# Two attention branches and a mixture of experts in one kernel: scores on halves of TensorE's array, masks of the maxima in 32x32 blocks, splits on GpSimd, tasks in another order

## The chip, the cores and the metric

One NeuronCore of a Trainium2 chip runs the whole program. The metric is the time of one execution on the device in microseconds. Its engines are called as in the profile: PE (TensorE, matmuls) with PEld (its weight loads), DVE (VectorE), ACT (ScalarE), POOL (GpSimd) and SP (SyncE, which here only issues DMAs). Each engine runs its own list of instructions in order; semaphores tie the lists together.

## The reference

The input x is 32 sequences of 256 rows of 128 float32. Two branches start from the layer norm of x and are added to x:

```python
xn = _layernorm(x)
# branch one: 16 heads of 8, causal, with biases
scores = jnp.einsum('bhqd,bhkd->bhqk', q, k) / SCALE
scores = jnp.where(causal_mask, jnp.float32(-1000000000000.0), scores)
attn = jnp.einsum('bhqk,bhkd->bhqd', softmax(scores), v); ... attn @ Wm + bm
# branch two: rmsnorm, 16 heads of 64 (32 of them rotated, keys from a latent of 16), causal
att = jnp.einsum('bhqd,bhkd->bhqk', q, k) / jnp.sqrt(jnp.float32(D))
y = softmax(att) @ v @ Wo; x1 = xn + y
# and behind it, on the rmsnorm of x1, a mixture of experts: top 2 of 8, plus a shared one
out = x + branch_one + (x1 + shared + routed)
```

Both softmaxes need the largest score of each query, so the scores are computed twice: once for their maximum and once for the exponential, the maximum then being taken off by two more rows of the contraction.

## The kernel before

A *block* is one sequence of 256 rows; there are 32 (`NB`). A loop over `c` runs from -1 to NB + 2, and in each turn over twelve *steps* `k`. In turn c PE makes the maxima's scores of block c + 1 and the exponentials' scores of block c: steps 0 to 5 are the six units of branch one, steps 6 to 11 the six of branch two. A unit (`UNITS`) is a pair of a 128-key tile and a 128-query tile for eight heads, 128 x 1024 scores in two PSUM banks; four of six are diagonal and need the causal mask. MX (`psm`) is the one buffer for the maxima, EX (`pse`) the one for the exponentials.

What each engine does in a step:

- PE: `max_unit` into MX (after DVE has read the last one, semaphore s_mr), some task, `exp_unit` into EX (after ACT's exponential of the last one, s_pt), more tasks; after every third step 24 matmuls `pv_half` of probabilities and values into PV (`psv`), which already use four column quarters of the array.
- DVE: the maximum over MX, which also transposes in 32x32 blocks (`max_unit`, L734), and tasks.
- ACT: the exponential of EX into PT (L1100), and ahead of a diagonal unit it writes the mask into EX, a bank at a time (a *seed*, L1106, semaphore s_sd counts them), on which the scores are then accumulated; and tasks.
- POOL and SP: tasks and DMAs.

The tasks are all the rest: projections of block c + 2 (`prep_*`), normalisation and output of block c - 1 (`norm`, `tail_in`, `tail_out`), and the experts for pairs of blocks (`moe_*`), so that even and odd turns differ. Their place is written out by hand as `if k == ...` in each engine's loop, the same for all turns. Three PSUM banks `ps0` to `ps2` are given out in turn (`claim`); `arrived` and `released` wait for a bank to be filled or freed.

Numbers are carried in parts. Branch one splits q and k in three bf16 parts, stacked as 48 rows of the contraction: `qsA`, `ksA` are [98, 16 heads, 256], of which 48 rows are parts, 48 are zeros and two carry the maximum. One matmul per head is 128 keys by 128 queries, eight per unit. Branch two uses float32r and two parts: `qsB` [128, 16, 256] holds high and low parts of the queries; a unit is, per bank, one 512-column product with the keys' high part (`ks1`, or `ksm` with 32 extra rows that mask a diagonal tile in the maxima) and one with their low part (`ks2`). The maxima of branch two go by 32 queries and all heads (`WIDE`). The mask of branch one's maxima is a matmul of an identity and the mask, 512 columns per bank, on four units of six (`mask`).

DVE splits the keys (`prep_ks`) and the experts' input (`moe_split`); POOL copies the keys into ksm (`prep_km`). The stacks of A and B are made by a write to DRAM and reads from it (`stack_a`, `stack_b`, `read_b`).

Of the kernel before, what the change touches and what calls it, by code (L numbers as in the profile page):

```python
# [14 lines left out]
H = 16  # L15
# [6 lines left out]
WIDE = [(0, 0), (0, 2), (0, 4), (0, 6), (1, 4), (1, 6)]  # L22
# [24 lines left out]
def build(nc, I, out, NB):  # L47
    with ExitStack() as ctx:
# [3 lines left out]
        def sem(name):  # L52
# [8 lines left out]
        qsA = [sb(f"qsA{i}", [98, H, S], BF16) for i in range(2)]  # L61
        ksA = [sb(f"ksA{i}", [98, H, S], BF16) for i in range(2)]
        qsB = [sb(f"qsB{i}", [128, H, S], F32R) for i in range(2)]
        ks1 = [sb(f"ks1{i}", [98, S], F32R) for i in range(2)]
        ksm = sb("ksm", [128, 4, 128], F32R)
        same = sb("same", [32, S], F32R)
        ks2 = [sb(f"ks2{i}", [98, S], F32R) for i in range(2)]
# [5 lines left out]
        R1 = [sb(f"R1{i}", [128, H, 4]) for i in range(2)]  # L73
        negm = [sb(f"negm{i}", [128, 32]) for i in range(2)]
# [7 lines left out]
        kcs = sb("kcs", [96, 2, S])  # L82
# [6 lines left out]
        wkk = sb("wkk", [128, 2, 192], F32R)  # L89
# [18 lines left out]
        kt_ = sb("kt_", [96, 2, S])  # L108
# [22 lines left out]
        scrA = [nc.dram_tensor(f"scrA{i}", (3, 2, 128, S), BF16).ap() for i in range(2)]  # L131
# [9 lines left out]
        d_mk = sem("d_mk")  # L141
# [18 lines left out]
        s_half, s_zq, s_zk, s_k1, s_ksi, s_wa, s_wn, s_wb, s_sa, s_sb = (  # L160
            sem(n) for n in ("s_half", "s_zq", "s_zk", "s_k1", "s_ksi", "s_wa", "s_wn", "s_wb", "s_sa", "s_sb"))
# [9 lines left out]
        sqk, sx, skk = stage[:, 0:256], stage[:, 256:768], stage[:, 768:960]  # L171
# [40 lines left out]
        def _(e):  # L212
# [15 lines left out]
            def scores(br, b, bk, u, i, K, start):  # L228
# [3 lines left out]
                if br == 0:  # L232
                    for j in range(4):
                        h = h0 + 4 * i + j
                        t = mm(bk[:, i, 128 * j:128 * j + 128], ksA[s][0:K, h, keys], qsA[s][0:K, h, queries], start and j == 0, True)
                else:
                    o = bk[:, i].rearrange("p (h q) -> p h q", h=4)
                    r = qsB[s][0:K, h0 + 4 * i:h0 + 4 * i + 4, queries]
                    mm(o, ks1[s][0:K, keys], r, start, False)
                    t = mm(o, ks2[s][0:K, keys], r, False, True)  # L240
                return t

            def wide_scores(b, u, i):

                s, (kt, q0) = b % 2, WIDE[u]
                keys, queries = slice(128 * kt, 128 * kt + 128), slice(32 * (q0 + i), 32 * (q0 + i) + 32)
                o = MX[:, i].rearrange("p (h q) -> p h q", h=H)
                if kt == q0 // 4:
                    mm(o, ksm[:, (q0 + i) % 4], qsB[s][:, :, queries], True, False)
                else:  # L250
                    mm(o, ks1[s][0:96, keys], qsB[s][0:96, :, queries], True, False)
                return mm(o, ks2[s][0:96, keys], qsB[s][0:96, :, queries], False, True)

            def max_unit(br, b, u):
                g = unit(br, b, u)
                if g >= 1:
                    w.wait_ge(s_mr, g)
                if br == 0:
                    if b or u >= 3:
                        w.wait_ge(d_ar[b % 2], 192 * (b // 2 + 1))  # L260
                    else:
                        w.wait_ge(d_a0, 192)
                else:
                    for hh in range(2):
                        w.wait_ge(d_br[b % 2][hh], 112 * (b // 2 + 1))
# [1277 lines left out]
```

## Time and profile before

| | us |
|---|---|
| median of 3 runs | 1465.03 (1463.62 to 1465.06) |
| the profiled execution | 1464.32 |
| its span, first to last instruction | 1462.3 |
| busy: PE, DVE, ACT, POOL | 1376.2, 1146.6, 997.3, 587.5 |
| mean granted clock of PE | 0.978 of full |
| DMA | 155.86 MB, mean 107 GB/s |

A span is measured from the first to the last instruction of the program, the execution's own time has a little around it. Busy time is the union of an engine's instructions; since matmuls overlap, how often PE issues them is read from the distance of their starts in the timeline, not from their durations.

### The profile page before, as it was taken

The page shows a single profiled execution, that of the slowest core. Times are in us where ns is not written, and L with a number is a line of the kernel's source. Part 1 is how long each engine was busy: PE and PEld are TensorE (multiplying, and loading weights), DVE is VectorE, ACT ScalarE, POOL GpSimd, SP SyncE. Part 2 cuts the span into 40 slices and gives each one's busy share as a digit, 9 for nine tenths or more (in the row PEclk, how much of TensorE's full clock was granted, in tenths as well). Part 3 has the DMA queues.
Part 4 walks back from the last instruction along what each step waited for, and adds up shares of the span by engine and source line. Part 5 has one row for each costly group of instructions (what it writes and reads, how often), then busy time and mean ns, then how long its engine had stood idle before and what let it go on. Part 6 is the DMA issues. An engine that isn't in the chain of part 4 may idle for free.

```text
span 1462.3 us, 36231 instructions
## 1 busy us (share of the span) xinstructions
PE 1376.2 (94%) x14438; PEld 1073.2 (73%) x14438; DVE 1146.6 (78%) x2358; ACT 997.3 (68%) x1585; POOL 587.5 (40%) x610
## 2 busy tenths in 40 slices
PE   4689999999999999999999999999999999999985
PEld 3467777777877777787777777777777777777653
DVE  7877797978879797987979788797879879787613
ACT  2156777767777777777777777777776777777762
POOL 5323434354433434443343445334344534433112
PEclk9589999999999999999999999999999999999997
DMA  6666655645465565556556545655655465555100
GB/s 161 122 124 122 122 118 108 129 100 115 85 129 116 115 120 107 115 91 118 115 114 119 112 110 96 112 120 113 116 114 113 102 101 119 116 106 115 17 3 14
DMA packets 136677, 155.86 MB, mean 107 GB/s; under 512 B 32687, under 2 KB 126543, under 8 KB 127391
## 3 DMA queue, kind: packets, MB, share of 16 engines
q1 hardware_dynamic: 118078, 151.97, 51.5%
q10 hardware_dynamic: 18432, 1.58, 1.6%
q8 instruction: 115, 1.88, 0.6%
q14 instruction: 52, 0.42, 0.1%
HBM read 82.79 MB, written 67.11 MB: 103 GB/s over the span
## 4 chain that ended last, share of the span: by engine, by line
PE 69%; DVE 18%; ACT 8%; issue 4%; POOL 0%; DMA 0%; ACTq 0%; DVEq 0%
PE ps L217 22%; PE psm L217 16%; PE pse L217 15%; PE psv L217 10%; DVE R L734 5%; ACT PT L1100 3%; DVE rt L796 2%; PE ps L325 2%; ACT pse L1106 2%; DVE th L846 1%; PE ps L391 1%; DVE xs L662 1%; ACT th L1179 1%; DVE th L858 1%; ACT th L1148 1%
## 5 line engine op out<-in xcount | busy, mean ns | idle before, releaser
L734 DVE TRANSPOSE_TENSOR_REDUCE R<-psm 128x32 f32<-128x1024 f32 x384 | 478.7, 1247 | 133.3 <-PE psm L217 132.2
L1100 ACT ACTIVATE PT<-pse 128x1024 f32<-128x1024 f32 x384 | 392.3, 1022 | 210.4 <-PE pse L217 210.3
L1106 ACT ACTIVATE pse<-maskb 128x512 f32<-128x512 bf16 x510 | 285.4, 592 | 16.9 <-ACT PT L1100 6.2
L217 PE MATMUL pse<-qsB,ks 98*128 98x512 f32 x768 | 215.0, 402 | 8.0 <-ACT pse L1106 7.8
L1296 POOL TENSOR_TENSOR ts_<-ts_,pA 128x512 f32<-128x512 f32 x32 | 37.2, 1162 | 445.8 <-DVE pA L668 445.8
L217 PE MATMUL psm<-qsB,ks 96*128 96x512 f32 x512 | 180.6, 414 | 6.0 <-DVE R L734 6.0
L217 PEld LDWEIGHTS pse<-qsB,ks 98*128 98x128 f32 x768 | 137.1, 189 | 58.6 <-issue 18.9
L1304 POOL TENSOR_TENSOR tc_<-tc_,ts_ 128x512 f32<-128x512 f32 x64 | 82.3, 1286 | 190.4 <-DVE ts_ L688 190.4
L217 PE MATMUL pse<-qsA,ksA 98*128 98x128 bf16 x1536 | 127.0, 220 | 9.7 <-ACT pse L1106 8.4
L217 PEld LDWEIGHTS psm<-qsA,ksA 96*128 96x128 bf16 x1536 | 96.3, 100 | 51.9 <-issue 27.7
L217 PE MATMUL psm<-qsA,ksA 96*128 96x128 bf16 x1536 | 120.9, 223 | 13.3 <-DVE R L734 12.6
L217 PEld LDWEIGHTS pse<-qsA,ksA 98*128 98x128 bf16 x1536 | 94.8, 98 | 39.8 <-ACT PT L1100 16.4
L217 PE MATMUL psm<-qsB,ksm 128*128 128x512 f32 x256 | 110.9, 433 | 9.5 <-DVE R L734 9.5
L217 PEld LDWEIGHTS psm<-qsB,ks 96*128 96x128 f32 x512 | 94.5, 192 | 22.0 <-DVE R L734 7.5
L1334 POOL TENSOR_TENSOR hT<-th,cbs 128x512 f32<-128x512 f32 x64 | 81.9, 1280 | 70.3 <-ACT cbs L1168 69.2
L1116 ACT ACTIVATE OT<-psv 128x512 f32<-128x512 f32 x128 | 76.5, 598 | 46.7 <-PE psv L217 46.7
L217 PE MATMUL ps<-xs,wqx 128*128 128x256 f32 x576 | 95.5, 303 | 8.0 <-DVE wqx L868 7.3
L1309 POOL TENSOR_TENSOR pB<-tc_,pB 128x1024 fp32r<-128x1024 f32 x32 | 76.2, 2380 | 58.4 <-ACT pB L1090 58.4
L217 PE MATMUL psv<-PT,vA 128*9 128x128 f32 x3072 | 97.1, 275 | 0.0
L217 PE MATMUL psv<-PT,vB 128*17 128x128 f32 x3072 | 96.4, 274 | 0.0
L217 PEld LDWEIGHTS ps<-xs,wqx 128*128 128x128 f32 x576 | 82.0, 196 | 15.7 <-DVE wqx L868 7.5
L217 PEld LDWEIGHTS psv<-PT,vB 128*17 128x17 f32 x3072 | 78.4, 97 | 15.5 <-issue 12.3
(194 smaller groups left out, 2623.7 us busy)
## 6 DMA issues: line engine op xcount, KB each, us to landing
scrB<-pB SPq DMA_DIRECT2D x32, 1536.0 KB, 6.0
qsB<-scrB SPq DMA_DIRECT2D x384, 128.0 KB
scrA<-pA SPq DMA_DIRECT2D x32, 384.0 KB, 2.8
qsA<-scrA SPq DMA_DIRECT2D x186, 64.0 KB
ksA<-scrA SPq DMA_DIRECT2D x186, 64.0 KB
xs<-in_x SPq DMA_DIRECT2D x16, 256.0 KB, 9.0
out<-zz SPq DMA_DIRECT2D x16, 256.0 KB, 4.7
qsB<-same SPq DMA_DIRECT2D x64, 16.0 KB
```

The source lines that it names most:

```text
L217: return e.matmul(o, l, r, start=start, stop=stop, skip_group_check=True)
L325: t = e.transpose(bk[:, c:c + 128], OT[n % 2][:, 256 * a + 128 * qt:256 * a + 128 * qt + 128], ident[:])
L391: t = e.transpose(bk[:, c:c + 128], BT[:, qt, 128 * a:128 * a + 128], ident[:])
L734: e.tensor_reduce(red, MX[:].rearrange("p i (c q) -> p (i c) q", q=32), AX.X, ALU.max, apply_transpose=True).then_inc(s_mr, 1)
L796: e.tensor_tensor(DD, L, bl(rs[:, 3], 8), ALU.subtract).then_inc(s_dd, 1)
L1100: e.activation(PT[g % 4], EX[:], ACT.Exp, scale=(8.0 ** -0.5, 0.125)[br]).then_inc(s_pt, 1)
L1106: e.activation(EX[:, i].rearrange("p (h q) -> p h q", h=4), bc(maskb[:], 4), ACT.Copy).then_inc(s_sd, 1)
L1116: e.activation(OT[n % 2][:], PV[:], ACT.Copy).then_inc(s_ot, 1)
L1296: e.tensor_tensor(rA[:], fA[:], pA[:, 0], ALU.subtract).then_inc(s_ra, 1)
L1304: e.tensor_tensor(tc_[:, a], tc_[:, a], ts_[:, a], ALU.add).then_inc(s_tr, 1)
L1309: e.tensor_tensor(pB[:, 1, 1:3], rot, pB[:, 0, 1:3].bitcast(F32), ALU.subtract).then_inc(s_pb2, 1)
L1334: e.tensor_tensor(hT[:, f, :], th[f % 2][:], cbs[f % 2][:], ALU.mult).then_inc(s_h, 1)
```

## The change

- **Branch one.** `qsA` and `ksA` become [128, 8, 256]: heads of one bank stand on rows 0 to 49, those of the other on rows 64 to 113, the zeros are gone. `pair_scores` issues, for each of four head positions, one matmul on rows 0.. into bank 0 and one on rows 64.. into bank 1. The number of matmuls and their 128 columns stay. `exp_one` waits for both seeds ahead of its first matmul.
- **Masks of the maxima.** The two 512-column matmuls with a full identity become eight with 32x32 pieces of it, 32 x 4 x 32 each: only the diagonal 32x32 blocks are masked. What lies above them is masked after the maximum, by two additions of a table `later` in DVE's `join_max`.
- **Branch two.** `ks1` and `ksm` get 128 rows (keys' high part twice, for both parts of q), with the extra rows in gaps. The low products contract over 48 rows, those of bank 0 on rows 0.., of bank 1 on rows 64... In a step PE now issues `max_two`, `exp_two` (high products), then `max_low`, `exp_low`. The maxima go by 64 queries and eight heads per bank; on a diagonal tile the high product is two matmuls of 256 columns a bank.
- **POOL** takes the sum of `kt_`, the split of the keys and `moe_split` from DVE; `prep_km` is two copies of 48 rows.
- **DMAs.** Stack A is written by four and read by 16 DMAs a block (one and 12 before); branch one's row of maxima goes out in four DMAs from ACT (two before).
- **Order.** Nearly all tasks have other places. `pv_half(1, c - 1, 1)` goes ahead of the first scores of a turn, the others behind the step's tasks.

```diff
+            def pair_scores(b, bk, u, K, start):
...
+                for j in range(4):
+                    for i in range(2):
+                        rows = slice(64 * i, 64 * i + K)
+                        t = mm(bk[:, i, 128 * j:128 * j + 128], ksA[s][rows, h0 // 2 + j, keys], qsA[s][rows, h0 // 2 + j, queries],
+                               start and j == 0, True)
+            def max_one(b, u):
...
+                if diagonal:
+                    w.wait_ge(s_wa, WMASK)
                     for i in range(2):
+                        o = MX[:, i].rearrange("p (h g q) -> p h g q", h=4, g=4)
+                        for j in range(4):
+                            r = slice(32 * i, 32 * i + 32)
+                            mm(o[32 * j:32 * j + 32, :, j, :], identb[r, r], bc(maskb[r, r], 4), True, True)
+                pair_scores(b, MX, u, 48, not diagonal).then_inc(s_mx, 1)
+            def exp_one(b, u):
...
+                if diagonal and g:
+                    w.wait_ge(s_sd, 2 * seeds(g))
+                pair_scores(b, EX, u, 50, not diagonal).then_inc(s_ex, 1)
+            def max_two(b, u):
...
+                    if kt == q0 // 2:
+                        for j in range(2):
+                            mm(o[:, :, j, :], ksm[:, 2 * (q0 % 2) + j], r[:, :, j, :], j == 0, False)
+                    else:
+                        mm(MX[:, i].rearrange("p (h q) -> p h q", h=8), ksm[:, 4], qsB[s][:, 8 * i:8 * i + 8, 64 * q0:64 * q0 + 64], True, False)
+            def exp_two(b, u):
...
+                for i in range(2):
+                    if kt == qt:
                         w.wait_ge(s_sd, 2 * seeds(g) - 1 + i)
+                    h = 8 * i + h0 // 2
+                    mm(EX[:, i].rearrange("p (h q) -> p h q", h=4), ks1[s][:, 128 * kt:128 * kt + 128],
+                       qsB[s][:, h:h + 4, 128 * qt:128 * qt + 128], kt != qt, False)
+            def low_products(b, bk, kt, heads, queries):
+                s = b % 2
+                for i in range(2):
+                    r, h = slice(64 * i, 64 * i + 48), slice(8 * i + heads.start, 8 * i + heads.stop)
+                    t = mm(bk[:, i].rearrange("p (h q) -> p h q", h=heads.stop - heads.start), ks2[s][r, 128 * kt:128 * kt + 128],
+                           qsB[s][r, h, queries], False, True)
...
             def join_max(br, b):
                 w.wait_ge(s_mr, unit(br, b, 5) + 1)
+                if br == 0:
+                    w.wait_ge(d_w[2], 64)
+                    e.tensor_tensor(R0[0][:, :, 0:4], R0[0][:, :, 0:4], bc(later[:], H), ALU.add)
+                    step(e.tensor_tensor(R1[0][:], R1[0][:], bc(later[:], H), ALU.add))
+                    after()
...
+            def prep_ks(b):
...
+                step(e.tensor_copy(ks1[s][0:112, :], kt_[:, 0]))
+                e.tensor_tensor(ks2[s][:], kt_[:, 0], ks1[s][0:112, :].bitcast(F32), ALU.subtract).then_inc(s_ks, 1)
...
+                    if k == 9:
+                        if body:
+                            pv_half(1, c, 0)
                         if even and moe:
                             moe_g(p, 0)
```

PE around steps 4 to 6 of an even turn, before. `ps<-ident,OT` are the transposes of `norm`, `wqx` those of `prep_rope`, `wvA` of `prep_v`:

```order
L217 MATMUL psm<-qsA,ksA 128x128 x7
L217 MATMUL psm<-maskb,identb 128x512 x2
L217 MATMUL ps<-xs,wqx 128x256 [waits s_free0]
L217 MATMUL ps<-xs,wqx 128x256 x5
L217 MATMUL pse<-qsA,ksA 128x128 [waits s_sd,s_pt]
L217 MATMUL pse<-qsA,ksA 128x128 x3
L217 MATMUL pse<-qsA,ksA 128x128 [waits s_sd]
L217 MATMUL pse<-qsA,ksA 128x128 x3
L217 MATMUL ps<-wvA,xs 128x256 [waits s_free2]
L217 MATMUL ps<-wvA,xs 128x256 x3
L217 MATMUL psm<-qsB,ksm 128x512 [waits s_ks,d_br11,s_km,d_br10,s_mr]
```

And now:

```order
L221 MATMUL ps<-wvA,xs 128x256 x3
L221 MATMUL psm<-maskb,identb 32x4x32 [waits s_mr]
L221 MATMUL psm<-maskb,identb 32x4x32 x7
L221 MATMUL psm<-qsA,ksA 128x128 x8
L221 MATMUL pse<-qsA,ksA 128x128 [waits s_sd,s_pt]
L221 MATMUL pse<-qsA,ksA 128x128 x7
L221 MATMUL ps<-xs,wqx 128x256 [waits s_free0]
L221 MATMUL ps<-xs,wqx 128x256 x5
L221 MATMUL psm<-qsB,ksm 128x8x32 [waits d_br11,s_km,d_br10,s_mr]
```

The projection that stood between the maxima's and the exponentials' scores of step 5 is now behind both, `prep_v` ahead of both, and the second wait for a seed is gone.

PE in steps 7 and 8 of the same turn, before:

```order
L217 MATMUL pse<-qsB,ks 128x512 [waits s_pt]
L217 MATMUL pse<-qsB,ks 128x512 x3
L217 MATMUL ps<-xs,wqx 128x256 [waits s_free2]
L217 MATMUL ps<-xs,wqx 128x256 x5
L411 MATMUL ps<-ident,th 128x128 [waits s_x2,s_free1]
L411 MATMUL ps<-ident,th 128x128 x3
L325 MATMUL ps<-ident,OT 128x128 [waits s_ot,s_free0]
L325 MATMUL ps<-ident,OT 128x128 x3
L217 MATMUL psm<-qsB,ks 128x512 [waits s_mr]
```

And now (`psm<-qsB,ks` is `max_low`; of `pse<-qsB,ks` the first two rows are `exp_two`, the last `exp_low`):

```order
L439 MATMUL ps<-ident,th 128x128 x3
L221 MATMUL psm<-qsB,ksm 128x512 [waits s_mr]
L221 MATMUL psm<-qsB,ksm 128x512
L221 MATMUL pse<-qsB,ks 128x512 [waits s_sd,s_pt]
L221 MATMUL pse<-qsB,ks 128x512 [waits s_sd]
L221 MATMUL psm<-qsB,ks 128x512 x2
L221 MATMUL pse<-qsB,ks 128x512 x2
L353 MATMUL ps<-ident,OT 128x128 [waits s_ot,s_free2]
```

The low products of both buffers stand together at the end of the step, and one high product stands behind each wait for a seed where two matmuls stood before.

POOL in an even turn, before, from `moe_x` to `prep_rlo`:

```order
L1328 TENSOR_TENSOR rs<-rs,half 128x4 [waits s_ms]
L1329 TENSOR_TENSOR th<-yy,rs 128x512 [waits s_g]
L1273 TENSOR_TENSOR sm<-sm,half 128x2 [waits s_st2]
L1304 TENSOR_TENSOR tc_<-tc_,ts_ 128x512 [waits s_free0,s_g]
L1315 COPY ksm<-ks 96x512 [waits s_mx]
L1309 TENSOR_TENSOR pB<-tc_,pB 128x1024 [waits s_pb1]
```

And now:

```order
L1374 TENSOR_TENSOR rs<-rs,half 128x4 [waits s_ms]
L1375 TENSOR_TENSOR th<-yy,rs 128x512 [waits s_g]
L1334 TENSOR_TENSOR tc_<-tc_,ts_ 128x512 [waits s_free0]
L1359 COPY ksm<-ks 48x512 [waits s_mx]
L1360 COPY ksm<-ks 48x512 [waits s_g]
L1368 TENSOR_TENSOR zz<-zz,yy 128x256 [waits s_y,s_free1,s_km]
L1370 TENSOR_TENSOR zz<-zz,crow 128x256 [waits s_g]
L1334 TENSOR_TENSOR tc_<-tc_,ts_ 128x512 [waits s_free0]
L1379 CAST x<-aT 128x512 [waits s_free1]
L1380 TENSOR_TENSOR x2lo<-aT,x 128x512 [waits s_g]
L1343 TENSOR_TENSOR kt_<-kt_ 112x256 [waits s_free2]
L1339 TENSOR_TENSOR pB<-tc_,pB 128x1024 [waits s_pb1]
```

The two rotations, the tail and the experts' split (`x`, `x2lo`) now follow each other in this stretch.

## Rows read from the trace of the kernel before

**Rows 1.** The page: busy times, TensorE's granted clock, the chain by engine.
```profile
PE 1376.2 (94%) x14438; PEld 1073.2 (73%) x14438; DVE 1146.6 (78%) x2358; ACT 997.3 (68%) x1585; POOL 587.5 (40%) x610
...
PEclk9589999999999999999999999999999999999997
...
PE 69%; DVE 18%; ACT 8%; issue 4%; POOL 0%; DMA 0%; ACTq 0%; DVEq 0%
```
**Rows 2.** Who waited for whom: total us, times, the longest.
```profile
ACT PT L1100 <- PE pse L217: 210.3, 273, 12.6
...
DVE R L734 <- PE psm L217: 132.2, 121, 2.7
...
PE psm L217 <- DVE R L734: 28.1, 34, 5.4
```
**Rows 3.** Timeline of PE: start, us to the end, instruction, count, [idle before].
```profile
404.51 2.18 PE L217 MATMUL ps<-hT,wds 64*128 64x512 f32 x4
...
489.37 0.69 PE L217 MATMUL ps<-hT,wds 64*128 64x512 f32 x1
```
**Rows 4.** Timeline of PE in steps 4 to 6, 9, and a mask.
```profile
423.25 0.61 PE L325 MATMUL ps<-ident,OT 128*128 128x128 f32 x4
423.69 0.61 PE L217 MATMUL psm<-qsA,ksA 96*128 96x128 bf16 x8
424.14 0.60 PE L217 MATMUL psm<-maskb,identb 128*128 128x512 bf16 x2
...
425.91 0.72 PE L217 MATMUL ps<-wvA,xs 128*128 128x256 f32 x4
...
427.95 1.17 PE L217 MATMUL pse<-qsB,ks 98*128 98x512 f32 x4 [0.25 <-ACT pse L1106]
...
439.28 1.08 PE L217 MATMUL pse<-qsB,ks 98*128 98x512 f32 x4
440.29 1.51 PE L217 MATMUL psv<-PT,vB 128*17 128x128 f32 x48
441.73 0.51 PE L217 MATMUL psm<-qsB,ksm 128*128 128x512 f32 x1
442.07 0.40 PE L217 MATMUL psm<-qsB,ks 96*128 96x512 f32 x1
...
713.68 0.60 PE L217 MATMUL psm<-maskb,identb 128*128 128x512 bf16 x2
714.11 0.60 PE L217 MATMUL ps<-wmA,aT 128*128 128x128 f32 x4
```
**Rows 5.** Groups of instructions: busy us, mean ns, idle before them.
```profile
L1106 ACT ACTIVATE pse<-maskb 128x512 f32<-128x512 bf16 x510 | 285.4, 592 | 16.9 <-ACT PT L1100 6.2 <-issue 1.2
...
L217 PEld LDWEIGHTS psm<-qsA,ksA 96*128 96x128 bf16 x1536 | 96.3, 100 | 51.9 <-issue 27.7 <-DVE R L734 20.6
...
L217 PEld LDWEIGHTS psm<-qsB,ks 96*128 96x128 f32 x512 | 94.5, 192 | 22.0 <-DVE R L734 7.5
L1304 POOL TENSOR_TENSOR tc_<-tc_,ts_ 128x512 f32<-128x512 f32 x64 | 82.3, 1286 | 190.4 <-DVE ts_ L688 190.4
...
L217 PEld LDWEIGHTS psv<-PT,vB 128*17 128x17 f32 x3072 | 78.4, 97 | 15.5 <-issue 12.3
...
L738 DVE TENSOR_TENSOR R<-R 128x64 f32<-128x64 f32 x64 | 25.5, 399 | 2.2
...
L721 DVE TENSOR_TENSOR ks<-kt_,ks 96x256 fp32r<-96x256 f32 x32 | 13.5, 421 | 1.1
```
**Rows 6.** Timeline of ACT: step 2 with the row's DMAs, and step 5.
```profile
416.19 1.02 ACT L1100 ACTIVATE PT<-pse 128x1024 f32<-128x1024 f32 x1
...
417.33 1.12 ACT L1106 ACTIVATE pse<-maskb 128x512 f32<-128x512 bf16 x2
...
426.17 1.00 ACT L1100 ACTIVATE PT<-pse 128x1024 f32<-128x1024 f32 x1
427.21 1.12 ACT L1106 ACTIVATE pse<-maskb 128x512 f32<-128x512 bf16 x2
```

More of the change, by code:

```diff
@@ L287, in exp_unit @@
                     w.wait_ge(s_pt, g)
[L288 removed]
+                w.wait_ge(d_c[0], 64 * (b + 1))
                 diagonal = UNITS[u][0] == UNITS[u][1]
[L290 to L294 removed]
+                if diagonal and g:
+                    w.wait_ge(s_sd, 2 * seeds(g))
@@ L525, in _ @@
                             setup_row()
+                    now += 0.5
+                    if k == 0 and body:
+                        join_max(1, c)
                     if k == 1:
-                        if soon:
-                            prep_x(n2)
-                        if odd and moe:
-                            moe_c(p)
-                        if before:
-                            norm(1, c - 1, 1)
-                    if k == 2:
+                        if even and done:
+                            moe_d(p - 1, (2, 3))
                         if before:
@@ L537, in _ @@
                             moe_g(p, 4)
-                    if k == 3 and before:
-                        tail_out(c - 1)
-                    if k == 4 and soon:
-                        prep_nope(n2)
-                    if k == 5 and soon:
-                        prep_rope(n2, 0)
-                    if k == 6 and n1 < NB:
-                        join_max(0, n1)
-                    if k == 8 and odd and moe:
-                        moe_g(p, 2)
+                    if k == 2:
+                        if even and done:
+                            moe_t(p - 1)
+                        if soon:
+                            prep_qk(n2)
+                        if before:
+                            tail_out(c - 1)
@@ new lines, in _ @@
+                    if k == 3:
+                        if n1 < NB:
+                            prep_k2(n1)
+                        if soon:
+                            prep_nope(n2)
+                        if body:
+                            pv_half(0, c, 0)
+                    if k == 4 and body:
+                        norm(0, c, 0)
+                    if k == 5 and odd and moe:
+                        moe_sel(p, 0)
+                    if k == 6:
+                        if body:
+                            pv_half(0, c, 1)
+                        if n1 < NB:
+                            join_max(0, n1)
@@ L613, in _ @@
                             moe_d(p, (4, 0))
+                        if even and moe:
+                            moe_c(p)
         @block.vector
@@ L1254, in _ @@
+                        if even and moe:
+                            moe_c(p)
         @block.gpsimd
```

620 lines of the change are left out of this document (311 added, 309 removed).

## The prediction

> **What bounds the kernel now.** I read the page first. PE is busy 94% of the 1462.3 us span, DVE 78%, ACT 68%, POOL 40%, and the chain of waits that ended last lies on PE for 69% [rows 1]. The granted clock is at 2.4 GHz in nearly all slices, so it is no term here. The waits view then says who waits: ACT for PE 210 us before the exponentials, DVE for PE 132 us before the maxima, PE before its maxima only 28 us for DVE [rows 2]. So TensorE sets the pace, and ACT and DVE follow with some slack. The timeline gives the period: two equal places two blocks apart start at 404.51 and 489.37, so a block takes 42.4 us [rows 3]; there are 32, with a short start and end around them. I work per block and multiply by 32.
>
> Matmuls overlap, so I go by the distance of starts. Eight branch-one matmuls of 128 columns take 0.45 us (423.69 to 424.14), 0.056 each; two 512-column mask matmuls 0.43 (713.68 to 714.11), 0.22 each; a 512-column one of branch two 0.235 (four in 1.01 at 439.28, with a hole of 0.07 to 0.09 at the end, below), one of 256 columns half of that, 0.118 [rows 4].
>
> **The change part by part.**
>
> *Scores of branch one.* A block has 96 of them (12 steps of 8), 96 x 0.056 = 5.4 us. They now contract over 48 or 50 rows, and each two stand in different halves of the array with different banks. Bounds: the two of a pair run together (48 x 0.056 = 2.7 us, saving 2.7) or one after the other (saving nothing). No row shows row halves. The nearest one shows column quarters: 48 matmuls of PV take 1.44 us (440.29 to 441.73), 0.030 each, where the same kind unpacked takes 0.11 (four OT transposes 423.25 to 423.69) [rows 4]; so four did run together. I take together: -2.7.
>
> *Masks of the maxima.* Four steps a block have two 512-column matmuls, 4 x 0.43 to 0.44 = 1.76 us. Now eight of 32x128 each in eight different blocks of the array. By PV's 0.030 each that is 0.24 a step, and if all eight stream together little over 0.06. I take 0.15: -1.76 + 0.6 = -1.2 (bounds -0.8 and -1.5).
>
> *Low products of branch two.* A block has 24 (ks2), 24 x 0.235 = 5.6 us; in pairs 12 x 0.235 = 2.8 if together. -2.8 (bound: 0). The high products keep their columns: on the four diagonal maximum steps four of 256 (0.47) stand for two of 512 (0.47).
>
> Sum of matmul work: -6.7 us.
>
> *Switches.* This is what the change pays with. Whenever the array goes from whole to parts or back, the trace shows a hole. Four of 512 columns before PV take 1.01 instead of 0.94 (439.28 to 440.29), and PV's twelve rounds of four, at OT's 0.11 a round, take 1.32 of its 1.44 [rows 4]. So 0.07 to 0.12; I take 0.09 each way, and the same for row parts as for column parts. In the order a block now has some 34 such changes against 9: each of six branch-one steps has full to (mask to) pairs to full, each of six branch-two steps full to low pairs to full. 25 x 0.09 = +2.3 us. The page "TensorEngine Tiling (Array Packing)" of the Trainium skill, Key Properties, says that a change of tiling mode, not of tile, drains the engine. By that rule masks (32x32) and pairs (64x128) are two modes and pay a change between them, which no row here shows; without it the sum would be 4 x 0.09 = 0.4 us better.
>
> *Loads uncovered.* After a hole the first weight load is not hidden. After PV the step from ksm to ks takes 0.34 instead of 0.24 (441.73 to 442.07): 0.10 [rows 4]. Loads of bf16 are short and add about 0.01. Entries into full mode with a 4-byte load and into low pairs rise from 3 to some 18 a block: +1.6. The second load of a low pair may stand behind the first: 6 x 0 to 0.11; I take +0.3. Together with the switches: +4.2, so PE's own work falls by 2.5 us.
>
> *Waits on ACT.* EX is one buffer: last score matmul, exponential, two seeds, next scores. The trace has it bare: last matmul of a step at 425.85 (0.056 before 425.91), exponential at 426.17, seeds from 427.21, each 0.59 and the two in 1.12, PE goes on at 427.95, 0.15 after the first seed [rows 4 to 6]. That is 2.1 us for one seed and 2.6 for both. Branch one waited for one seed before its first four matmuls; now it waits for both before the first pair. And branch two has but one 0.235 matmul behind the first seed, where it had two: the second seed comes 0.53 after the first, so 0.3 is waited. Against this stand the fillers between one exponential step and the next, which shrink with PE's work. From the order and the durations above:
> Step 4 to 5 (OT, wvA, mask, pairs, three changes) 1.8 us against 2.6: 0.8 waited, 0 before. Step 5 to 6: 1.4 in one block, 1.6 in the other, against 2.1 + 0.3: 0.9 and 0.7, before 0.47 and 0.25. Step 8 to 9: 2.1 against 2.2 + 0.3: 0.4, before 0.1. Step 1 to 2 in odd blocks 0.3, and PV now stands before the first scores of a block, where it can wait 0.25 in even blocks. Sum some 2.3 a block. The same places and the wait for moe_split cost before some 1.3. So +1.0. ACT also issues four DMAs for branch one's row between exponential and seeds, where it had two; with these two the seeds begin 0.12 behind the exponential's end (416.19 + 1.02 to 417.33), without them 0.04 (426.17 + 1.00 to 427.21) [rows 6]: +0.1.
>
> *DVE, POOL and SP.* A block takes the kt_ sum, the ks cast and subtraction (256 columns each, 421 ns for the last) and half of moe_split's two passes over 512 from DVE, and gives it two additions of `later` at 399 each: about -1 us on an engine with 1146.6 / 32 = 35.8 [rows 1, 5]. PE waits little for it, so I price this at nothing; it keeps DVE as covered in a shorter block as it is now. POOL takes these over at up to 1286 for 512 columns [rows 5] and copies ksm in four pieces instead of two: +4 to +6 us on an engine with 18.4 of 42.4. Queued behind each other in even blocks, from step 6 on, are r1, moe_x, rope, two ksm copies, tail, rope and the split, nine times 512 columns, at most 11.6 us; moe_g(p, 0), which waits for the split, comes near step 9.7, 3.7 steps of 3.4 us later. So it is just hidden. If it is late by 1 us, PE waits 16 us in all. SP issues 20 DMAs for the A stack where it had 13, the last of them near step 10, two steps before that stack is read; hidden.
>
> **Sum.** -6.7 + 4.2 + 1.0 + 0.1 = -1.4; I give 0.3 back, for fillers that end in a wait for one of the ps banks. -1.1 a block x 32 = -35 us. The profiled execution took 1464.3 us, 2.0 more than its span; less 35 it is 1429, and as it stands 0.7 under the median of the runs, 1430 us for the median. Bounds: masks at -1.5, no stagger, 0.5 of waits instead of 1.0 give -2.5 a block, 1385; masks at -0.8, full stagger, 2 of waits and nothing to spare give +0.7, 1487.
>
> **The rivals.**
> A. *Both waits and changes are cheaper.* For it: a hole costs nothing where PE would wait for ACT anyway, and the new order puts work before the maxima. Against it: the three short fillers above. -1.8 to -2.9 a block: 1372 to 1407.
> B. *Slower: the weight loads of a pair come one after the other and set the pace.* Each pair needs two loads. Were a load as long as a matmul's 0.056, a pair would take 0.112 and branch one would save nothing: -1.1 + 2.7 = +1.6 a block, 1516. It decides from a load of 0.04 on, where 48 x (0.08 - 0.056) = 1.1 is lost and nothing is left. Against it: the record of a 128-column bf16 load is 100 ns, that of a 17-column 4-byte one 97, and 128 columns of 4 bytes take 192 [rows 5], so bf16's 128 columns cost no more than 17 of the others, a small part of 0.056. The Trainium skill ("TensorE: Matmul & The Clock Gate", Weight-path perf modes) gives the fast weight load four times in theory and about two as measured; by an estimate from that page a load would at two take some 53 ns, and B would hold. By that rule the trace agrees with four rather than two: 100 against 192 ns with the fixed part of a record in both.
> C. *Slower by waits:* ACT's chain of 2.6 us bare in five more steps of the twelve, or POOL late with ks or the split. +1.2 to +2 a block over my sum: 1468 to 1495.
> D. *The halves don't overlap at all.* 2.7 + 2.8 + 0.6 are lost, the added waits of 1.0 go with them: +4 a block, 1593. PV's quarters speak against it.
> E. *It comes out even,* the waits taking what the pairs give: within 0.2%, 1462 to 1468.
>
> **How the numbers follow.** Forecast (1407 to 1455) 0.45, A 0.22, between 1455 and 1462 0.06, E 0.06, B 0.06, C 0.11, D 0.04. Faster by over 0.2%, which is about what a measurement of this kernel can tell from none (the three runs lie within 1.4 us), 0.73; same 0.06; slower 0.21. For 8 in 10 I leave out D, B's upper part and A's lower end: 1380 to 1490.
>
> **What would show it.** Right: starts of the branch-one matmuls in pairs a few ns apart and 0.056 from pair to pair; the low pairs 0.24 apart; PE's busy time 80 us lower; holes of 0.09 to 0.2 around each; PE idle before pse ended by ACT's seeds at least twice as long as now, most of it at steps 4 to 5 and 5 to 6; DVE busy near 1116, POOL near 715. Wrong: eight branch-one matmuls still in 0.45 (B or D); holes near zero or 0.2 even for bf16; a new wait of PE for POOL (ks, ksm or x2lo), which I priced at nothing; a block period over 42.4.

## The result, and the profile after

The changed kernel takes 1547.6 us (median of 4 runs, 1539.6 to 1548.4) where the kernel before, on the same chip, takes 1464.3 (1463.5 to 1465.1). The ratio is 1.056, 95% interval 1.052 to 1.059. The forecast was 1430 (1380 to 1490): a gain of 35 us was forecast and a loss of 83 came. From the page of the changed kernel, beside [rows 1]:

```profile
PE 1360.3 (88%) x15462; PEld 954.7 (62%) x15462; DVE 1116.2 (72%) x2293; ACT 978.2 (63%) x1583; POOL 717.3 (46%) x804
...
PEclk9979899999999999899898999989898999999888
...
PE 69%; ACT 13%; DVE 5%; ACTq 5%; issue 4%; SPq 1%; DMA 1%; POOL 1%; POOLq 0%; DVEq 0%
```

DVE and POOL are busy for 1116 and 717 us, where 1116 and 715 were forecast; that VectorE's number fits is partly chance, as is shown below. What is new is ACTq in the chain, 5% where it had none. ACTq is ScalarE's own issue of DMAs. The waits view, beside [rows 2]:

```profile
DVE R L766 <- PE psm L221: 271.5, 173, 10.9
ACT PT L1128 <- PE pse L221: 251.4, 228, 10.7
...
ACT pse L1134 <- issue: 75.8, 31, 2.8
PE pse L221 <- ACT pse L1134: 74.6, 95, 1.7
```

ScalarE stood 31 times, once a block and 2.4 us each, before it wrote the seeds (L1134), for "issue", that is for nothing but its own instruction stream. The timeline of all engines shows one of these in step 7 (the same columns as [rows 3]):

```profile
733.14 1.28 POOL L1334 TENSOR_TENSOR tc_<-tc_,ts_ 128x512 f32<-128x512 f32 x1 [0.30 <-DVE ts_ L732]
733.29 1.17 DVE L784 CAST cA<-negm 128x32 bf16<-128x32 f32 x1
...
734.10 1.02 ACT L1128 ACTIVATE PT<-pse 128x1024 f32<-128x1024 f32 x1 [2.27 <-PE pse L221]
...
734.50 0.53 DVE L787 TENSOR_TENSOR cA<-negm,cA 128x32 bf16<-128x32 f32 x1
...
735.06 2.43 ACTq L1167 DMA_DIRECT2D qsA<-cA  x4
...
737.53 1.12 ACT L1134 ACTIVATE pse<-maskb 128x512 f32<-128x512 bf16 x2 [2.41 <-issue]
...
738.28 0.94 PE L221 MATMUL pse<-qsB,ks 128*128 128x512 f32 x2 [1.31 <-ACT pse L1134]
```

Two things are read from it. The four DMAs take 2.43 us of ScalarE, 0.61 each. And they begin 0.96 us behind the exponential's start, since the row cA is not ready: its cast, over 128x32, takes 1.17 us and ends when GpSimd's addition ends (733.14 + 1.28 = 734.42), and the low part behind it takes 0.53. So the seeds stand 3.43 us behind the exponential's start, against 1.04 in a plain step [rows 6], and PE goes idle.

Behind such a stop the clock falls. Two stretches of the changed kernel, one before and one behind this stop (start and end in us, length, busy us of PE, PEld, DVE, ACT, POOL, then the granted clock as a share of 2.4 GHz, DMA share, GB/s):

```profile
725.00:737.00 12.00, 10.87 (x125) 7.74 (x123) 10.74 (x21) 6.53 (x12) 8.72 (x11) 1.00 0.19 44
739.00:749.30 10.30, 10.30 (x75) 7.06 (x75) 8.70 (x22) 5.02 (x8) 8.41 (x10) 0.50 0.46 145
```

One microsecond behind the stop the clock is at 1.2 GHz and stays there for 10 us, with PE busy all the time. Summed over the span, TensorE had 1.2 GHz for 199 us, against 63 before; after the first 100 us it is 183 against 22.

### The profile page after: what moved, and what is told of

Read it like the earlier page. It is cut to its first block, busy times and chain, and to the rows that moved or that the text cites. A ratio compares the mean times of both kernels' runs of the same rounds, so it can differ in the third digit from the quotient of the medians.

```text
span 1545.6 us, 38750 instructions
## 1 busy us (share of the span) xinstructions
PE 1360.3 (88%) x15462; PEld 954.7 (62%) x15462; DVE 1116.2 (72%) x2293; ACT 978.2 (63%) x1583; POOL 717.3 (46%) x804
## 4 chain that ended last, share of the span: by engine, by line
PE 69%; ACT 13%; DVE 5%; ACTq 5%; issue 4%; SPq 1%; DMA 1%; POOL 1%; POOLq 0%; DVEq 0%
PE ps L221 21%; PE psm L221 14%; PE pse L221 14%; PE psv L221 13%; ACT PT L1128 6%; ACT pse L1134 5%; ACTq L1167 5%; PE ps L353 3%; DVE R L766 1%; ACT OT L1144 1%; PE ps L419 1%; DVE xs L706 1%; PE ps L344 1%; SPq L1481 1%; ACT th L1178 1%
## 5 line engine op out<-in xcount | busy, mean ns | idle before, releaser
L766 DVE TRANSPOSE_TENSOR_REDUCE R<-psm 128x32 f32<-128x1024 f32 x384 | 478.1, 1245 | 273.0 <-PE psm L221 271.5
L1134 ACT ACTIVATE pse<-maskb 128x512 f32<-128x512 bf16 x510 | 285.5, 592 | 86.7 <-issue 75.8
L221 PE MATMUL pse<-qsB,ks 128*128 128x512 f32 (+1 forms) x768 | 236.7, 445 | 56.2 <-ACT pse L1134 56.2
L221 PEld LDWEIGHTS pse<-qsB,ks 128*128 128x128 f32 (+1 forms) x768 | 112.2, 206 | 106.8 <-issue 77.7
L221 PE MATMUL psm<-qsB,ksm 128*128 128x256 f32 (+1 forms) x640 | 144.1, 341 | 35.1 <-DVE R L766 21.5
L1298 POOL TENSOR_TENSOR sm<-sm,half 128x2 f32<-128x2 f32 x32 | 22.9, 717 | 289.1 <-DVE sm L681 289.0
L221 PEld LDWEIGHTS psm<-qsB,ksm 128*128 128x128 f32 x640 | 101.4, 204 | 54.1 <-DVE R L766 36.4
L221 PE MATMUL psv<-PT,vB 128*17 128x128 f32 x3072 | 111.6, 301 | 2.2 <-ACT PT L1128 2.2
L221 PE MATMUL psm<-qsB,ks 48*128 48x512 f32 x384 | 105.8, 548 | 0.0
L353 PE MATMUL ps<-ident,OT 128*128 128x128 f32 x512 | 87.4, 297 | 10.2 <-ACT OT L1144 8.2
L221 PE MATMUL pse<-qsA,ksA 50*128 50x128 bf16 x1536 | 76.2, 218 | 20.7 <-ACT pse L1134 18.4
L221 PEld LDWEIGHTS psv<-PT,vA 128*9 128x9 f32 x3072 | 79.3, 92 | 20.3 <-issue 14.7
L221 PEld LDWEIGHTS ps<-xs,wqx 128*128 128x128 f32 x576 | 80.2, 200 | 16.2 <-DVE wqx L899 6.6
```

The costliest lines, as they stand in the source:

```text
L221: return e.matmul(o, l, r, start=start, stop=stop, skip_group_check=True)
L353: t = e.transpose(bk[:, c:c + 128], OT[n % 2][:, 256 * a + 128 * qt:256 * a + 128 * qt + 128], ident[:])
L766: e.tensor_reduce(red, MX[:].rearrange("p i (c q) -> p (i c) q", q=32), AX.X, ALU.max, apply_transpose=True).then_inc(s_mr, 1)
L1134: e.activation(EX[:, i].rearrange("p (h q) -> p h q", h=4), bc(maskb[:], 4), ACT.Copy).then_inc(s_sd, 1)
L1298: e.tensor_tensor(sm[:, 1, c], sm[:, 0, c], half[:, 0:2], ALU.pow).then_inc(s_pw1, 1)
```

## The experiments

All times are medians over the runs, ratios are to the kernel before on the same chip.

**1. Where does the row's issue hurt?** Four kernels. The first puts the row's DMAs (called with br = 0) behind the exponential of step 9; the second gives all four to SyncE's queue; the third two to ScalarE and two to SyncE; the fourth is the kernel before with each of its two row DMAs cut in two.

```
@@ r9: ScalarE (the same for the first turn, which has no exponential)
-                        exp_unit(br, c, u, ... (0, n1) if k == 7 and n1 < NB else None)
+                        exp_unit(br, c, u, ... (0, n1) if k == 9 and n1 < NB else None)
@@ s4: ScalarE, exp_unit                           @@ s4: SyncE, step 7 (row_one issues the four)
-                if row:                          +                    if k == 7 and c + 1 < NB:
+                if row and row[0] == 1:          +                        row_one(c + 1)
                     max_row(*row)
```

> The changed kernel with one edit: ACT issues the four DMAs of branch one's row behind the exponential of step 9, where no seed follows, and not behind that of step 7, ahead of two seeds. Theory W (the issues are the loss): in the changed kernel the four issues begin 0.9 us behind the exponential of step 7, take 0.62 us each and hold the seeds 2.5 us, so PE stands still about 2 us once a block and falls to 1.2 GHz after it; with the hold gone, seeds of step 7 follow 0.05 us behind the exponential, 32 x 2.2 = 70 us go, half-clock time falls from 199 us toward before's 63, and the whole is 1400 to 1440 us. Rival M (the array's changes of mode and the new order are the loss): the span stays above 1500 us, since all holes and fillers are as they were. Rival C (the clock falls for another reason): the period shortens by 2 us but half-clock time stays near 199 us, 1470 to 1480.

> The changed kernel, the four DMAs of branch one's row issued by SP behind its reads of stack A instead of by ACT. W: as the run with the row at step 9 or 5 to 10 us better, because ACT's queue issues nothing for this row: 1390 to 1435 us. If the row came late for the next block's first scores, PE would wait at step 0 instead and this run would be slower than the one at step 9. M: above 1500 us.

> The changed kernel, ACT issues two of the four DMAs at the old place in step 7 and SP the other two. Tells the number of issues from the lateness of the row: W with number alone (0.62 each): seeds 1.25 us earlier than in the changed kernel, so 32 x 1.25 = 40 us and some clock, 1480 to 1500 us. If the lateness of DVE's cA (0.9 us behind the start of the exponential) is most of it, 1510 to 1530. M: no change, 1540 to 1550.

> The kernel before with one edit: the two DMAs of branch one's row are split by heads into four, same bytes, same place. W: before, the row is ready when the exponential of step 7 begins, so 1.0 of 2.5 us of issues lies beside it and some of the rest is PE's slack there; seeds 1.2 us later, PE waits about 0.6 to 1.2 us a block: 1485 to 1505 us. M and C: within 0.5% of before, 1465.

Measured: r9 1497.1 (ratio 1.022, interval 1.020 to 1.024), s4 1484.7 (1.014, 1.010 to 1.017), h2 1494.5 (1.021, 1.019 to 1.022), b4 1495.9 (1.022, 1.020 to 1.024). So to take the issue, or half of it, out of that place was worth 50 to 63 us. h2 and b4 came as expected; r9 and s4 are 50 us and more above what theory W gave them, and the time at 1.2 GHz fell only from 199 us to 160.5 and 165.5. The kernel before, with nothing changed but two DMAs more on ScalarE, loses 32. Its timeline in step 7:

```profile
397.77 1.03 ACT L1100 ACTIVATE PT<-pse 128x1024 f32<-128x1024 f32 x1 [2.12 <-PE pse L217]
397.78 2.43 ACTq L1143 DMA_DIRECT2D qsA<-cA  x4
400.25 1.12 ACT L1106 ACTIVATE pse<-maskb 128x512 f32<-128x512 bf16 x2 [1.45 <-issue]
```

The DMAs are issued while the exponential runs: 1.03 us of them is free, the rest, 1.4, is not. Two DMAs hide under it (0.48 us each in the kernel before) and four don't. A fifth kernel, e3, shows the other side: the kernel before with its two row DMAs issued by SyncE takes 1463.4 (ratio 0.999, 0.998 to 1.000), where 1461 (1459 to 1464) was expected. The two cost it nothing that can be told. But s4 has none of this and is still 20 us above the kernel before; something else was lost.

**2. The cast that waits.** c1 is the changed kernel with two calls of VectorE's step 6 exchanged, so that the row is made before the rotation's products that GpSimd adds up.

```
                     if k == 6:
+                        if n1 < NB:
+                            max_row(0, n1)
                         if soon:
                             prep_rope(n2, 0)
-                        if n1 < NB:
-                            max_row(0, n1)
```

> The changed kernel with one swap on VectorE: in step 6 it makes the row of branch one (reduction, cast to cA, low part) ahead of the rotation products whose sum GpSimd takes, and not behind them. Theory W: in the changed kernel the cast to cA takes 1165 ns in the median where it took 182 before, and ends when GpSimd's addition tc_<-tc_,ts_ (1.27 us) ends, since that was under way when it began; so the row is ready 0.95 us behind the exponential's start, and ScalarE's four DMAs (2.43 us) begin there instead of at once. With the swap: cast 182 ns, the DMAs begin within 0.1 us of the exponential's start, the seeds about 2.5 us behind it instead of 3.43, 0.95 x 32 = 30 us off 1547.6, so about 1517 (1505 to 1525). Rival I: only the four DMAs' own time on ScalarE counts, and the row would be late anyway (by PE's transpose); the seeds stay about 3.4 us behind the exponential and the time within 5 us of 1547.

Measured: 1500.6 (ratio 1.025, 1.023 to 1.027), 47 us less than the changed kernel and 4 below the range expected. The cast by itself, in the changed kernel and in c1 (count, then ns minimum/median/maximum):

```profile
L784 DVE CAST cA<-negm x32: 182/1165/1173, 71.9 to 1446.4; 128x32 bf16<-128x32 f32 x32
```
```profile
L784 DVE CAST cA<-negm x32: 180/181/217, 70.1 to 1403.2; 128x32 bf16<-128x32 f32 x32
```

and ScalarE in c1's step 7:

```profile
708.42 1.03 ACT L1128 ACTIVATE PT<-pse 128x1024 f32<-128x1024 f32 x1 [2.28 <-PE pse L221]
708.43 2.49 ACTq L1167 DMA_DIRECT2D qsA<-cA  x4
710.97 1.12 ACT L1134 ACTIVATE pse<-maskb 128x512 f32<-128x512 bf16 x2 [1.52 <-issue]
```

As theory W said, the DMAs now begin with the exponential. Time at 1.2 GHz fell too (183 to 88 us after the first 100), and the gain shows in PE's busy time, 1360.3 to 1318.2 us for the same matmuls. PE's idle time stayed as it was: its waits for the seeds fell (74.6 to 58.8 us), those for VectorE's maxima rose (28.3 to 46.3).

**3. The routing that waits.** In s4 the timeline around step 9 of an even block reads:

```profile
374.95 0.73 POOL L1341 TENSOR_TENSOR kt_<-kt_ 112x256 f32<-112x256 f32 x1
...
375.08 2.99 DVE L829 SCALAR_TENSOR_TENSOR rt<-rt,pri 128x32 f32<-128x32 f32 x1
...
375.64 2.39 POOL L1337 TENSOR_TENSOR pB<-tc_,pB 128x1024 fp32r<-128x1024 f32 x1
...
378.66 1.24 DVE L766 TRANSPOSE_TENSOR_REDUCE R<-psm 128x32 f32<-128x1024 f32 x1
...
379.85 0.79 POOL L1317 TENSOR_SCALAR h<-xs,sm 128x128 f32<-128x128 f32 x1
...
379.95 0.61 PE L221 MATMUL psm<-qsB,ksm 128*128 128x256 f32 x2 [2.38 <-DVE R L766]
...
380.00 0.33 DVE L843 TENSOR_TENSOR rt<-rt,rs 128x32 f32<-128x32 f32 x1
380.37 0.19 DVE L845 TENSOR_TENSOR rt<-rt,pri 128x32 f32<-128x32 f32 x1
```

A routing operation over 32 columns, 0.19 us by itself, begins 0.13 behind a GpSimd addition and ends with the second one (375.64 + 2.39 = 378.03). The reduction behind it is late and PE stands 2.4 us, in 14 blocks. (The changed kernel has such holds too, on other routing operations, L827 and L833, 1.16 and 0.65 us in the mean; but there PE waits for the maxima no longer than before, 28.3 us against 28.1 [rows 2]. The routing's hold became a loss only when the row's was gone.) The kernel before has the same wait of 2.3 us in front of nothing urgent:

```profile
356.29 2.37 POOL L1309 TENSOR_TENSOR pB<-tc_,pB 128x1024 fp32r<-128x1024 f32 x1 [3.68 <-ACT pB L1090]
356.42 2.30 DVE L796 TENSOR_TENSOR rt<-rt,rs 128x32 f32<-128x32 f32 x1
```

The Trainium skill says it on "SBUF — State Buffer", Who interferes with whom: a VectorE instruction with two inputs in SBUF, or a copy or cast in one of its two-port modes, and a GpSimd instruction that reads SBUF shut each other out for the whole instruction. The trace agrees for GpSimd's two-input additions, in length (2.99 against 0.19), and in which ones wait: no reduction from PSUM (L766) of the changed kernel takes more than 1.25 us, whatever GpSimd does. It departs where GpSimd runs a TENSOR_SCALAR of 0.79 us (L1317): a two-input operation of VectorE begun 0.15 behind it (L843) took 0.33 us, 0.14 more than by itself, and not the whole rest; the next one (L845) took its 0.19. The measurement decides: not each such meeting lasts for the whole instruction. One thing it leaves to measurement: here VectorE, once shut out, waits through two GpSimd instructions in a row.

p1 moves the two GpSimd operations to the end of step 11; e1 leaves them in place in other blocks, but in even blocks gives the long one to VectorE, behind the reduction of step 9, and puts the short one at the end. e2 is e1 with the swap of c1.

```
@@ e1: VectorE, step 9, even                      @@ e1: GpSimd
                         if even and moe:         -                        if soon:
+                            if soon:             +                        if soon and not (even and moe):
+                                prep_rlo(n2)                                  prep_kt(n2)
                             moe_route3(p)                                     prep_rlo(n2)
```

> s4_row_sp with two GpSimd operations moved from step 9 to the end of step 11 (the sum into kt_, 0.73 us, and the low part of the rotated rows pB<-tc_,pB, 2.39 us). Theory W: in 14 of the even blocks VectorE's small routing operation rt<-rt,pri begins at 0.13 us behind kt_'s start and ends 0.05 us behind the end of pB (2.99 us instead of 0.19), so the reduction R queued behind it is 2.4 us late and PE stands 2.4 us in front of the next maxima (14 x 2.38 = 33 us). With both moved those waits of PE go, and part of the time at half the clock with them (104 us after the first 100, where before has 22): 1484.7 - 33 = about 1450 (1440 to 1460). Rival S: PE's hole is that of GpSimd's split of the experts' input being late, and the routing's long record an effect beside it; the hole stays and the time within 5 us of 1485. Rival L: the low part's late end delays the loads of branch two, and a new wait of PE for them gives back half or more, 1465 or above.

> s4_row_sp with, in blocks that route (even ones), the low part pB<-tc_,pB made by VectorE behind the reduction of step 9 and ahead of the routing's third part, and the sum into kt_ by GpSimd at the end of step 11; other blocks as before. GpSimd then has no large operation with two inputs under way while VectorE routes, and the scratch write of branch two starts about as early as in s4_row_sp (unlike p1_sp_rlo_late, where PE waited 100 us for the loads of branch two). Theory W: rt<-rt,pri 0.19 us instead of 2.99, PE's 14 waits of 2.38 us in front of the maxima of step 10 go (-33 us), and with them the stretches at half the clock that follow each (11 of 3.4 to 6.8 us, some 45 us, worth half: -15 to -20): about 1435 (1425 to 1448). Rival: VectorE's own 1.1 to 1.6 us more in step 9 or a new wait of the loads keeps PE standing over 1 us there, 1460 or above.

> e1_sp_rlo_vector with the swap of c1_row_before_rope: the cast to cA 182 ns instead of 1165, so VectorE's reduction of step 7 is 1.3 us earlier; with the row issued by SyncE nobody waits for the row itself. Theory: 0 to 8 us under e1, 1430 (1420 to 1440).

Measured: p1 1592.3 (1.087, 1.085 to 1.089), e1 1453.9 (0.992, 0.990 to 0.994), e2 1455.6 (0.994, 0.992 to 0.996). p1 went as rival L said, and much further: the low part is the last piece of the scratch write of branch two, and PE waited for its loads:

```profile
PE psm L221 <- DMA qsB<-scrB: 100.3, 20, 7.2
```

With the swap on top it was 1597.4. It is no test of W. e1 is: the routing operation is back at 192 ns in all 16 blocks, the waits of 2.38 are gone, 31 us against s4. It missed the 1435 (1425 to 1448) that I expected. One reason the trace shows: VectorE now carries 1.3 us more in step 9, and PE waits for it 14 times, 1.1 us each (the view of g1 below). e2, expected 0 to 8 us under e1, is 1.7 above it, within the noise. With e1 the changed layout is 0.6 to 1.0% faster than the kernel before.

**4. The four DMAs alone.** f2 is the changed kernel with both waits for GpSimd gone (the swap and e1's edit), and the DMAs on ScalarE.

> The changed kernel with the swap and with the low part by VectorE in even blocks, so e2_sp_rlo_vector_swap with the four DMAs of the row back on ScalarE, between exponential and seeds. Both waits for GpSimd are gone here; what is left over e2 is the four DMAs alone: they take 2.43 us from the exponential's start, which itself takes 1.02, so the seeds are 1.4 us late, x 32 = 45 us if all of it reaches PE; the same in the kernel before (b4_before_four) cost 32. Expect 1455.5 + 32 to 45: 1488 to 1500. If it is 1460 or less, it was the cast alone that made the DMAs dear.

Measured: 1489.4 (1.017, 1.014 to 1.020), 34 us over e2, as the 32 of b4 and as expected. Its waits, then PE's line on the pages of f2 and e2:

```profile
PE pse L221 <- ACT pse L1141: 59.3, 96, 1.5
ACT pse L1141 <- issue: 46.3, 31, 1.7
```
```profile
PE 1329.7 (89%) x15462; PEld 933.8 (63%) x15462; DVE 1084.9 (73%) x2307; ACT 978.6 (66%) x1583; POOL 693.1 (47%) x790
```
```profile
PE 1295.0 (89%) x15462; PEld 914.2 (63%) x15462; DVE 1105.9 (76%) x2307; ACT 981.4 (67%) x1583; POOL 691.6 (48%) x790
```

PE does the same matmuls in both and is busy 35 us longer in f2, while its idle time (span less busy) is 157 us against 160. So the loss of the four DMAs shows as slower matmuls: f2 has 121 us at 1.2 GHz after the first 100, e2 has 54.

**5. The start, and VectorE's order.** g1 is e1 with SyncE's first scratch write of branch two ahead of six loads of constant rows. f1 also does VectorE's expert work before the routing's third and fourth parts.

```
@@ g1: SyncE, start                               @@ f1: VectorE, step 10, even
             stack_a(0)                           +                            moe_hg(p, 0)
+            stack_b(0)                           +                            moe_route3(p)
             w.wait_ge(s_mk, 1)                                                moe_route4(p)
                                                  -                            moe_hg(p, 0)
```

> e1_sp_rlo_vector with one thing moved at the start of the program: SyncE issues the first scratch write of branch two before, not behind, the six loads of constant rows (same, one2). Theory: of the forecast's 35 us, e1 shows 10.4. Its blocks 4 to 29 take 21.2 us less than before (0.85 a block, forecast 1.1), but its first transposition of row maxima comes 11.3 us later than before (69.6 against 58.3), because SyncE, which issues 20 DMAs a block for branch one's stack instead of 13 and four more constant rows, reaches the first scratch write of branch two at 44.1 us instead of 34.2; PE stands 12.05 us before the first product of branch two. With the move the write goes out at 37.3: 6 to 7 us off, 1447 (1445 to 1450). Rival: the loads are bound by something else, no change.

> g1_start with, in even blocks, VectorE's work on the expert's first gate product (moe_hg(p, 0)) ahead of the routing's third and fourth parts instead of behind them. In e1 PE waits 1.1 us in 13 even blocks before moe_g(p, 1) for VectorE, which has the low part (1.29 us) in front of that work: 13 x 1.1 = 15 us, of which the next wait in line gives back about half. 1440 (1432 to 1446).

Measured: g1 1448.5 (0.989, 0.988 to 0.990), 5 us under e1, as expected. The write, in e1 and in g1:

```profile
44.09 0.52 SPq L1497 DMA_DIRECT2D scrB<-pB  x1
```
```profile
37.24 0.40 SPq L1497 DMA_DIRECT2D scrB<-pB  x1
...
61.54 1.19 PE L221 MATMUL psm<-qsB,ksm 128*128 128x256 f32 x4 [10.54 <-DMA qsB<-scrB]
```

f1 missed: 1453.1 (0.992, 0.989 to 0.994). The wait for VectorE before the gate product went, and one of 1.48 us in 14 blocks before the maxima of step 10 came; VectorE's queue is full there. With the swap as well it was 1455.2. g1 is the best version, 16 us under the kernel before and 99 under the changed one. That the 16 are the new layout's alone is not shown: of the repairs only the row on SyncE was tried on the kernel before (e3). Its page and waits:

```profile
PE 1294.5 (90%) x15462; PEld 915.1 (63%) x15462; DVE 1119.5 (78%) x2307; ACT 980.1 (68%) x1583; POOL 693.3 (48%) x790
```
```profile
PE pse L221 <- ACT pse L1141: 29.7, 60, 1.5
PE psm L221 <- DVE R L771: 26.1, 49, 3.2
...
PE ps L221 <- DVE th L882: 15.3, 14, 1.5
```

**6. Are the pairs worth their order?** e4 is e2 with the eight matmuls of a pair step issued as four on the upper half of the rows and then four on the lower.

```
-                for j in range(4):
-                    for i in range(2):
+                for i in range(2):
+                    for j in range(4):
```

> e2_sp_rlo_vector_swap with the eight score products of branch one as four on the upper half of the array's rows, then four on the lower (the order that q1_pairs_apart had; that run was bound by the loads of branch two and told nothing). What is paired side by side saves 4 x 0.056 us = 0.2 us a unit, 12 units a block: 2.4 us a block, 77 us where PE's own work sets the pace. Since steps 4 to 6 wait for ScalarE's seeds, about two thirds: +50 us (35 to 80) over e2. Rival: halves hardly overlap, within 5 us.

Measured: 1456.5 (0.995, 0.993 to 0.996), e2 within 1 us: my 50 us were wrong. The timeline of PE in e4:

```profile
713.02 0.41 PE L221 MATMUL psm<-qsA,ksA 48*128 48x128 bf16 x8
713.25 0.40 PE L221 MATMUL pse<-qsA,ksA 50*128 50x128 bf16 x8
```

Eight matmuls still take 0.23 us. The same order on top of p1 with the swap did as little (1597.3 against 1597.4). So the times do not tell whether the halves overlap. The starts in the trace do: in e4 eight begin at 713.021, .034, .087, .100, .143, .156, .199 and .212, two by two 13 ns apart, and not one by one every 29 ns as they would if each were only twice as quick. A rival, that 48 rows of contraction run faster than 96, has this against it in the trace of before too: products hT,wds over 64 rows and over 128 rows have records of the same length (0.69 and 0.59 us at 743.8, 0.70 and 0.59 at 744.9).

## Why the prediction was wrong, point by point

**Scores in pairs: right.** In the changed kernel, beside the 0.45 for eight in [rows 4]:

```profile
757.82 0.25 PE L221 MATMUL psm<-maskb,identb 32*32 32x128 bf16 x8
758.00 0.40 PE L221 MATMUL psm<-qsA,ksA 48*128 48x128 bf16 x8
758.24 0.39 PE L221 MATMUL pse<-qsA,ksA 50*128 50x128 bf16 x8
```

Eight scores in 0.24; in the trace they begin 3 ns apart within a pair and 52 to 57 from pair to pair. Masks: 0.18 a step against the 0.15 taken; the eight begin within 0.023 us of each other and the pairs 0.16 behind the last. D is out. B's two loads of 53 ns one after the other would have made 106 a pair. The factor of four that B cites is given for fp8 in the Trainium skill ("TensorE: Matmul & The Clock Gate", Weight-path perf modes); the loads here are bf16.

**Low products and holes: right in size.** Two low products begin together and the next work 0.33 to 0.34 us behind (733.32 to 733.66 in the timeline of step 7), 0.235 and a hole of 0.10. 0.09 was the price taken for a change between whole and parts. But this hole stands between two low pairs, where nothing changes, and the next one, before whole matmuls, is no longer (733.66 to 733.99). The runs don't separate the price of a change from that of a load.

**PE's own work: right.** It was to fall by 2.5 us a block, 80 in all. In g1 PE is busy 1294.5 us against 1376.2, 82 less. In the changed kernel itself it fell by 16 only, with 183 us at 1.2 GHz after the first 100 against 42 in g1.

**Waits on ACT in short steps: real, but too dear.** The sum had 2.3 us a block against 1.3 before, 32 us more. PE's waits for the seeds are 29.7 us in g1 and 16.2 before, so 0.9 a block against 0.5, 14 us more. In the changed kernel they are 74.6, with the four DMAs in them.

**The four DMAs at +0.1 a block: the step that failed.** I took from [rows 6] what two DMAs left over behind the exponential, 0.08 us, and priced two more at about as much. The step measured is 1.4 us: the two were free because they take 0.95 and fit under an exponential of 1.02; four take 2.43. f2 against e2: 34 us instead of 3.

**VectorE at nothing: failed too, and no rival named it.** Rival C had POOL late with its results. What came was POOL in VectorE's way, however early it was. The cast to cA fell behind the rotation's addition in 31 of 32 blocks. Together with the routing this is after minus f2, 1547.6 - 1489.4 = 58 us. c1 gives 47 for the cast with ScalarE waiting on it, and c1 minus f2 11 for the routing behind that; with the row out of the way the routing is worth 31 (s4 minus e1). VectorE's 1116 us, forecast to the number, hide this: in the changed kernel the 32 casts to cA take 36.3 us, 30 more than at their own 182 ns, and f2, without the holds and with the low part as well, has 1084.9. The trace of before had the sign of it: a mean of 399 ns for R<-R in [rows 5], an operation whose median there is 226. I priced two more of them by that mean and did not ask why it was so high; these additions of `later` took 225 and 218 ns.

**The clock "is no term here": failed.** It was no term in the kernel before, which has nothing at 1.2 GHz between 100 and 1390 us. All 22 such stretches of the changed kernel in that time begin within 5 us behind the start of a stop of PE of 1.1 to 2.1 us (it has 36 of over 1.1), and 18 of 19 in s4. f2 has 5 stops of over 1.1 us, but 15 of 0.76 to 0.87 before pse, where e2 has none; 11 of f2's 15 stretches begin 3.3 to 3.8 us behind one of these. Not each stop is followed by such a stretch. The matmuls of the changed kernel and its variants are the same, so their PE busy times tell what the clock adds (times are medians, busy and idle those of the profiled execution):

| | time, us | PE busy | PE idle | at 1.2 GHz after the first 100 us |
|---|---|---|---|---|
| before | 1464.3 | 1376.2 | 86 | 22 |
| before, four DMAs (b4) | 1495.9 | 1391.5 | 103 | 46 |
| changed | 1547.6 | 1360.3 | 185 | 183 |
| cast first (c1) | 1500.6 | 1318.2 | 184 | 88 |
| row on SyncE (s4) | 1484.7 | 1314.1 | 174 | 104 |
| both waits gone, four DMAs (f2) | 1489.4 | 1329.7 | 157 | 121 |
| both waits gone, row on SyncE (e2) | 1455.6 | 1295.0 | 160 | 54 |
| g1 | 1448.5 | 1294.5 | 150 | 42 |

Between the changed kernel and g1, 66 us are busy time and 36 idle time. This is an account of where the time shows, not two independent costs: matmuls at 1.2 GHz also fill waits that PE would have had.

**SyncE hidden: right in the loop, wrong at the start.** The first row maxima of branch two are transposed at 69.6 us in e1, at 58.3 before; g1 won back 6 of this in the trace and 5 in the time.

The rest between g1 and the forecast, 18 us, is in waits: PE's busy time fell as forecast, and its idle time rose by 63 us where the sum had 45. The seeds took 18 less than priced. Against that stand waits that no term of the sum has: 15 us for VectorE that g1's own edit brings (L882 above), 11 for VectorE's BT (16 times 0.7 us, 0.5 in all before), 8 for ScalarE's OT (0.2 before), and some 5 for the start that is still later than before (63.4 us). By the trace a block of g1 takes 41.6 us against 42.4 before, 0.8 less where 1.1 was forecast.

## What to carry to other kernels

A DMA's issue is an instruction of the engine that issues it: count them at their full length (0.5 to 0.6 us here) against the instruction that hides them, and not by what stuck out before. When work moves from VectorE to GpSimd, ask for each VectorE instruction with two SBUF inputs, and each small cast, which GpSimd instruction will be under way when it starts; free time on GpSimd is not free for VectorE. Read a small operation's minimum beside its mean: the difference is a wait that no waits view shows.

## What I had not expected of the hardware

- The issue order of matmuls on two row halves did not matter: four and four took 0.23 us for eight, as alternating did, and still began two by two (e4).
- A VectorE operation shut out by GpSimd waited through two of its instructions in a row, 2.99 us, and the waits view files all of it as busy time of VectorE.
- After many stops of PE of 0.8 to 2.4 us the clock was at 1.2 GHz for 3.4 to 10 us, mostly with PE fully busy; the kernel before has that nowhere between 100 and 1390 us. The four DMAs on ScalarE instead of SyncE (f2 against e2) cost 34 us in this way, without more idle time of PE.
